# Two rows to a partition: 4 MB slots and transfers, half of the bias kept in PSUM

## The chip, the cores and the metric

The kernel runs on one core of a Trainium2 chip. Such a core has TensorE (PE, the matmul engine), VectorE (DVE), ScalarE (ACT) and GpSimd (POOL), the queues SP and ACT that issue transfers, and 16 DMA engines between HBM (the chip's main memory) and SBUF (the core's working memory, 128 partitions). PSUM is the small memory that TensorE writes. The metric is device microseconds (us), the median of several runs. All arithmetic is fp32.

## The reference

```python
B, D, L = (16384, 4096, 6)
x0 = inputs
def step(x, wb):
    wi, bi = wb
    xw = jnp.matmul(x, wi)          # (B, D) by (D, 1)
    x_new = x0 * xw + bi + x
    return (x_new, None)
x, _ = jax.lax.scan(step, inputs, (w, b))
```

Every layer's result has the form `x0 * s + c`, where `s` is one number for each row and `c` one vector for all rows. So a row needs its six dot products with the six weight vectors, a recurrence of six steps on `1 + dot` (with constants from weights and biases), and one pass `out = x0 * s_last + c_last`, where `c_last` is the sum of the six biases. 268 MB are read and 268 MB written.

## The kernel before

**Tiles and units.** The 16384 rows are 128 tiles of 128 rows; a row lies in one partition, so a tile is 128 x 4096 fp32, 2 MB, with 16 KB for each partition. SBUF has eight tile slots. Work goes in units: the first two tiles alone (`HEAD`), then 61 pairs, then four tiles alone (`TAIL`).

**A unit's steps.** VectorE transposes its tiles in 32 x 32 squares into `blocks`, which has four places of 128 x 2048 (L264); a pair is four pieces of 2048 columns, two pieces for each half of D. TensorE multiplies each piece with the weights into `dots` (L401 for pairs, L359 for single tiles). ScalarE copies `dots` into `spread` (L197), TensorE folds it into `turned` (L370), ScalarE adds 1 (`growth`, L205), VectorE runs the six-step recurrence (L275), and VectorE finishes each tile in place with one instruction over 4096 columns (L286). ScalarE's queue then stores the tile (L210; the last tile in quarters, L236).

**Order of the work.** All order is written out by hand. VectorE, for a pair u: transposes of pieces 0 and 1, the recurrence of u-1, finish of u-1's first tile, transposes of pieces 2 and 3, finish of u-1's second tile (L310 to L323). ScalarE stores u-1's first tile before it spreads u's dots, the second behind it (L218 to L230). SP issues the loads in order; from the ninth on, each waits until the store of the same slot has landed (L141). DVE waits for both tiles of a pair (L266). A transpose waits until TensorE has used the piece that was in its place of `blocks` four pieces ago (L261).

**The start.** Weights and biases land in the last slot. TensorE sums the biases into `scratch` (four PSUM banks) in two rounds, `sum_bias(0)` and `sum_bias(1)` (L337), by a matrix `quarter_sum` that ScalarE builds; ScalarE copies each round into `c_last` in SBUF (L187). SP's load for the last slot waits until this is done.

## Time and profile before

| | us |
|---|---|
| median of 3 runs (1281.14 to 1282.9) | 1281.35 |
| the profiled execution: its own time | 1280.2 |
| its span in the profile | 1278.4 |
| busy: DVE / PE / ACT | 1150.2 / 780.7 / 102.7 |
| mean DMA rate over the span | 420 GB/s |
| TensorE clock granted (share of full speed) | 0.782 |

Busy time is summed over the instructions of an engine. The span begins with the first instruction and ends with the last event; what lies around it is 1.8 us here. The DMA share of a stretch is the mean busy share of the 16 DMA engines; it can read slightly above 1 since the records of two packets that follow each other overlap a little. A packet is the contiguous piece that one DMA engine moves as one record: here one row of 16 KB, or 4 bytes for the semaphore that tells of the landing.

### The profile page before, as it was taken

The numbers are of one execution on the slowest core, as the hardware profiler recorded it, in microseconds if no ns is written. First come the engines' busy times: TensorE is split into PE (matmuls) and PEld (weight loads), VectorE is DVE, ScalarE is ACT, GpSimd is POOL, SyncE is SP. The second block draws the span as 40 slices with busy tenths as digits, with TensorE's granted clock in tenths as the row PEclk, the third lists the DMA queues.
The fourth block names the chain that finished last, engine by engine and source line by source line (L and its number), as shares of the span: only waits on it lengthen the run. The fifth ranks groups of instructions, "written<-read, shape, count | busy, mean of one in ns | idle before, by whom it ended". The sixth has DMA issues, their size and how long they took to land.

```text
span 1278.4 us, 20057 instructions
## 1 busy us (share of the span) xinstructions
PE 780.7 (61%) x9114; PEld 728.6 (57%) x9114; DVE 1150.2 (90%) x526; ACT 102.7 (8%) x345; POOL 4.3 (0%) x17
## 2 busy tenths in 40 slices
PE   8666666555656655556555665665655665665653
PEld 4666566555556655555545565565655654665653
DVE  5999999898988988989889898898998988989896
ACT  3000000000000000000000000000000000000010
POOL 1000000000000000000000000000000000000000
PEclk9877787887877778778787777777777778678677
DMA  9999999999999999999999999999999999999996
GB/s 385 416 380 428 430 431 431 429 427 429 433 429 431 431 430 432 430 431 424 421 424 425 418 427 421 424 425 422 427 424 421 424 423 425 425 423 425 426 421 286
DMA packets 37385, 537.28 MB, mean 420 GB/s; under 512 B 4168, under 2 KB 4168, under 8 KB 4728
## 3 DMA queue, kind: packets, MB, share of 16 engines
q1 hardware_dynamic: 18432, 268.44, 50.1%
q10 hardware_dynamic: 18936, 268.64, 49.3%
q8 instruction: 7, 0.11, 0.0%
q14 instruction: 10, 0.08, 0.0%
HBM read 268.63 MB, written 268.44 MB: 420 GB/s over the span
## 4 chain that ended last, share of the span: by engine, by line
DMA 72%; DVE 15%; PE 8%; issue 3%; ACT 1%; DVEq 0%
DMA out_dram<-tiles 56%; DMA tiles<-in_r_inputs_dram 15%; DVE tiles L286 8%; DVE blocks L264 7%; PE dots L401 6%; ACT spread L197 1%; PE dots L359 1%; PE scratch L339 1%; DMA tiles<-in_L_rec_w_dram 0%; PE strips L334 0%; PE strips L349 0%; ACT c_last L189 0%; PE turned L370 0%; DVE scale L275 0%; DVEq L42 0%
## 5 line engine op out<-in xcount | busy, mean ns | idle before, releaser
L401 PE MATMUL dots<-blocks,weights 128*64 128x128 f32 x7808 | 662.6, 349 | 380.8 <-DVE blocks L264 380.6
L401 PEld LDWEIGHTS dots<-blocks,weights 128*64 128x64 f32 x7808 | 628.7, 185 | 405.3 <-DVE blocks L264 405.2
L264 DVE STREAM_TRANSPOSE blocks<-tiles 128x2048 f32<-128x2048 f32 x256 | 576.0, 2288 | 100.1 <-issue 100.1
L286 DVE SCALAR_TENSOR_TENSOR tiles<-tiles,scale,c_last 128x4096 f32<-128x4096 f32 (+1 forms) x131 | 571.9, 4368 | 0.2
L197 ACT ACTIVATE spread<-dots,group_mask 128x128 f32<-128x128 f32 (+1 forms) x268 | 75.2, 363 | 1062.6 <-PE dots L401 1020.3
L370 PE MATMUL turned<-layer_sel,spread 128*128 128x8 f32 x512 | 68.1, 258 | 85.5 <-ACT spread L197 85.5
L370 PEld LDWEIGHTS turned<-layer_sel,spread 128*128 128x128 f32 x512 | 62.3, 191 | 101.4 <-issue 95.6
L359 PE MATMUL dots<-blocks,weights 128*64 128x64 f32 x768 | 32.4, 266 | 11.0 <-DVE blocks L264 11.0
L359 PEld LDWEIGHTS dots<-blocks,weights 128*64 128x64 f32 x768 | 31.7, 180 | 12.9 <-issue 12.9
L205 ACT ACTIVATE growth<-turned,ones 128x16 f32<-128x16 f32 (+1 forms) x67 | 18.3, 273 | 85.0 <-PE turned L370 85.0
L275 DVE TENSOR_TENSOR_SCAN scale<-growth,cw 128x6 f32<-128x6 f32 x128 | 13.3, 142 | 8.9 <-ACT growth L205 8.9
L339 PE MATMUL scratch<-tiles,quarter_sum 24*128 24x512 f32 x16 | 10.7, 825 | 0.0
L339 PEld LDWEIGHTS scratch<-tiles,quarter_sum 24*128 24x128 f32 x16 | 4.0, 253 | 5.7 <-issue 4.8
L334 PE MATMUL strips<-tiles,copies 24*128 24x512 f32 x4 | 3.7, 1085 | 5.6 <-DMA tiles<-in_L_rec_w_dram 5.6
L291 DVE STREAM_TRANSPOSE tiles<-strips 128x1024 f32<-128x1024 f32 x1 | 1.2, 1249 | 5.5 <-PE strips L334 5.5
L334 PEld LDWEIGHTS strips<-tiles,copies 24*128 24x128 f32 x4 | 1.2, 318 | 6.6 <-issue 6.6
L189 ACT COPY c_last<-scratch 128x2048 f32<-128x2048 f32 x2 | 3.7, 1866 | 5.4 <-PE scratch L339 5.4
L302 DVE CUSTOM_DVE_ANT_0 tiles<-strips,tiles 24x1024 f32<-24x1024 f32 x1 | 1.2, 1212 | 2.7 <-PE strips L349 2.7
L349 PE MATMUL strips<-tiles,earlier 24*24 24x512 f32 x4 | 3.6, 1052 | 0.0
L183 ACT COPY weights<-tiles 32x768 f32<-32x768 f32 x2 | 3.0, 1520 | 4.6 <-DVE tiles L291 4.6
L349 PEld LDWEIGHTS strips<-tiles,earlier 24*24 24x24 f32 x4 | 0.5, 138 | 2.9 <-issue 2.9
L244 DVE MEMSET weights<- 128x2048 f32 x1 | 1.8, 1765 | 0.4 <-issue 0.4
(25 smaller groups left out, 11.3 us busy)
## 6 DMA issues: line engine op xcount, KB each, us to landing
tiles<-in_r_inputs_dram SPq DMA_DIRECT2D x128, 2048.0 KB, 14.9
out_dram<-tiles ACTq DMA_DIRECT2D x127, 2048.0 KB, 25.5
out_dram<-tiles ACTq DMA_DIRECT2D x4, 512.0 KB, 7.0
tiles<-in_L_rec_w_dram ACTq DMA_DIRECT2D x1, 96.0 KB
tiles<-in_L_rec_b_dram ACTq DMA_DIRECT2D x1, 96.0 KB
```

Source lines behind the costliest of these rows:

```text
L189: nc.scalar.copy(c_halves[:, :, h, :], scratch[:]).then_inc(scratch_copied, 1)
L197: nc.scalar.activation(spread[:, 0:n_of, :, g, :], dots[:, 0:n_of, :, :], ACT.Copy, scale=group_mask[:, g:g + 1]).then_inc(dots_spread, 1)
L205: nc.scalar.activation(growth[:, 0:n_of, :], turned[:, 0:n_of, :], ACT.Identity, bias=ones[:, 0:1]).then_inc(growth_ready, 1)
L264: nc.vector.transpose(blocks[:, p % PLACES, :], source).then_inc(blocks_ready, 1)
L275: nc.vector.tensor_tensor_scan(scale[:, u % 2, t, 0:L], growth[:, t, 0:L], cw[:, 0:L], 1.0, ALU.mult, ALU.add).then_inc(scale_ready, 1)
L286: nc.vector.scalar_tensor_tensor(out=tiles[:, s, at], in0=tiles[:, s, at], scalar=scale[:, u % 2, t, L - 1:L], in1=c_last[:, at], op0=ALU. ...
L334: nc.tensor.matmul(strips[:, k, :], copies[0:STRIPS, :, :], strips_w[:, k * BANK:(k + 1) * BANK], start=True, stop=True).then_inc(w_copied, 1)
L339: last = nc.tensor.matmul(scratch[:, j, :], quarter_sum[0:STRIPS, j, :], strips_b[:, h * BANK:(h + 1) * BANK], start=True, stop=True)
L349: nc.tensor.matmul(strips[0:STRIPS, k, :], earlier[0:STRIPS, 0:STRIPS], strips_b[:, k * BANK:(k + 1) * BANK], start=True, stop=True).then_ ...
L359: last = nc.tensor.matmul(dots[at:at + KM * Q, 0, :, :], weights[:, h * PIECE // Q + k:h * PIECE // Q + k + KM, :], blocks[:, p % PLACES, ...
L370: last = nc.tensor.matmul(turned[:, t, :], spread[:, t, m, :, :], layer_sel[:, m, :], start=(m == 0), stop=(m == KM - 1))
L401: last = nc.tensor.matmul(dots[at:at + KM * Q, :, :, :], weights[:, c * CH // Q + k:c * CH // Q + k + KM, :], place[:, :, k * Q:(k + KM) * Q],
```

## The change

A slot now holds two tiles: row 2p of a group of 256 rows lies in partition p beside row 2p+1. So partition p reads and writes 32 KB that are contiguous in HBM, and a pair is one load and one store of 4 MB. There are five slots of 4 MB in place of eight of 2 MB. To make room, `blocks` shrinks from four places to two, and of `c_last` only the lower half of the columns stays in SBUF (`c_low`); the upper half is left in `scratch` in PSUM (`c_high`) and read from there. The finish of a tile is therefore two instructions of 2048 columns. The six tiles that go alone are still loaded and stored alone, 16 KB to a partition. ScalarE stores a whole unit, behind the growth of the next one. The biases come by four small DMAs into the partitions where TensorE sums them with `ones` (no `quarter_sum`), and `strips_b` comes last.

```diff
-PLACES = 4
+PLACES = 2
+PIECES_OF_PAIR = 4
-N_SLOTS = 8
+N_SLOTS = 5
...
+    x_pairs = x.rearrange("(q p t) d -> q p t d", p=P, t=TB)
+    out_pairs = out.rearrange("(q p t) d -> q p t d", p=P, t=TB)
+    b_halves = b.rearrange("l (h j n) -> j l h n", h=2, j=G)
...
-        tiles = sb("tiles", [P, N_SLOTS, D])
+        tiles = sb("tiles", [P, N_SLOTS, TB, D])
-        c_last = sb("c_last", [P, D])
+        c_low = sb("c_low", [P, HALF])
+        c_high = scratch[:].rearrange("p j n -> p (j n)")
...
+            for q in range(n_all_pairs):
+                s = q % N_SLOTS
+                if q == N_SLOTS - 1:
                     sp.wait_ge(weights_ready, G)
-                    sp.wait_ge(scratch_filled, 2)
+                    sp.wait_ge(bias_summed, 2)
                     sp.wait_ge(strips_summed, 1)
...
+                if q >= N_SLOTS:
+                    for t in range(TB if in_singles(q - N_SLOTS) else 1):
+                        sp.wait_ge(y_stored[s][t], 16 * transfers(q - N_SLOTS, t))
+                if in_singles(q):
+                    for t in range(TB):
+                        sp.dma_start(tiles[:, s, t, :], x_pairs[q, :, t, :]).then_inc(x_landed[s][t], 16)
+                else:
+                    sp.dma_start(tiles[:, s, :, :], x_pairs[q]).then_inc(x_landed[s][0], 16)
...
             act.dma_start(strips_w, w_strips).then_inc(w_landed, 16)
-            act.dma_start(strips_b, b_strips).then_inc(b_landed, 16)
...
+                act.dma_start(b_rows[j * Q:j * Q + L, :, :], b_halves[j]).then_inc(b_landed[j], 16)
+            act.dma_start(strips_b, b_strips).then_inc(strips_b_landed, 16)
...
+            act.wait_ge(bias_summed, 1)
+            nc.scalar.copy(c_low[:], c_high).then_inc(c_low_ready, 1)
...
             for u in range(1, n_units):
...
-                    store(first)
-                    spread_dots(u)
-                    for t in range(1, n_of):
-                        store(first + t)
-                    make_growth(u)
+                spread_dots(u)
+                make_growth(u)
+                store(u - 1)
...
-                parts = 1 if n < n_tiles - 1 else PIECES
+                parts = 2 if n < n_tiles - 1 else STORE_PARTS
...
+                    c = c_low[:, at] if i < parts // 2 else c_high[:, i * width - HALF:(i + 1) * width - HALF]
+                    done = nc.vector.scalar_tensor_tensor(out=tile[:, at], in0=tile[:, at],
+                                                          scalar=scale[:, u % 2, t, L - 1:L], in1=c,
+                                                          op0=ALU.mult, op1=ALU.add)
```

The first listing is the ACT queue before: from the first stores on through one pair of the long middle part (L210 stores, L197 spreads, L205 makes the growth).

```order
L205 ACTIVATE growth<-turned,ones 128x8
L210 DMA out_dram<-tiles 128x4096 x2
L197 ACTIVATE spread<-dots,group_mask 128x4x32 x4
L205 ACTIVATE growth<-turned,ones 128x16
L210 DMA out_dram<-tiles 128x4096
L197 ACTIVATE spread<-dots,group_mask 128x4x32 x4
L210 DMA out_dram<-tiles 128x4096
L205 ACTIVATE growth<-turned,ones 128x16
```

The second is the same place now: L223 stores a single tile, L221 a pair.

```order
L212 ACTIVATE growth<-turned,ones 128x8
L223 DMA out_dram<-tiles 128x4096
L202 ACTIVATE spread<-dots,group_mask 128x4x32 x4
L212 ACTIVATE growth<-turned,ones 128x16
L223 DMA out_dram<-tiles 128x4096
L202 ACTIVATE spread<-dots,group_mask 128x4x32 x4
L212 ACTIVATE growth<-turned,ones 128x16
L221 DMA out_dram<-tiles 128x8192
```

The store of tile 1 has moved behind the spread and the growth of the first pair, and each pair's two stores are one, behind the next unit's growth.

The third listing is DVE before, one pair of the middle part (L264 transposes, L275 the recurrence, L286 finishes).

```order
L264 STREAM_TRANSPOSE blocks<-tiles 128x2048 x2
L275 SCALAR_TENSOR_TENSOR scale<-growth,cw 128x6 x2
L286 SCALAR_TENSOR_TENSOR tiles<-tiles,scale,c_last 128x4096
L264 STREAM_TRANSPOSE blocks<-tiles 128x2048 x2
L286 SCALAR_TENSOR_TENSOR tiles<-tiles,scale,c_last 128x4096
```

And DVE now, the same pair (`scratch` is the upper half of the bias in PSUM).

```order
L268 STREAM_TRANSPOSE blocks<-tiles 128x2048 x2
L279 SCALAR_TENSOR_TENSOR scale<-growth,cw 128x6 x2
L291 SCALAR_TENSOR_TENSOR tiles<-tiles,scale,c_low 128x2048
L291 SCALAR_TENSOR_TENSOR tiles<-tiles,scale,scratch 128x2048
L268 STREAM_TRANSPOSE blocks<-tiles 128x2048 x2
L291 SCALAR_TENSOR_TENSOR tiles<-tiles,scale,c_low 128x2048
L291 SCALAR_TENSOR_TENSOR tiles<-tiles,scale,scratch 128x2048
```

The order of transposes and finishes stays; each finish has become two instructions, the second with an operand in PSUM.

## Rows read from the trace of the kernel before

**Rows 1.** Windows: stretch, busy us by engine, TensorE clock, DMA share, GB/s.

```profile
0.00:5.00 5.00, 0.00 (x0) 0.00 (x0) 2.56 (x5) 1.53 (x2) 3.71 (x14) 1.00 0.52 187
...
2.00:36.00 34.00, 29.16 (x290) 16.78 (x290) 19.25 (x16) 11.62 (x20) 3.03 (x8) 1.00 0.99 410
60.00:90.00 30.00, 18.99 (x230) 17.60 (x228) 30.00 (x14) 2.83 (x10) 0.00 (x0) 0.82 0.95 374
160.00:560.00 400.00, 242.94 (x2792) 229.86 (x2792) 364.21 (x165) 28.57 (x101) 0.00 (x0) 0.78 1.01 430
560.00:1240.00 680.00, 409.92 (x4721) 388.24 (x4723) 615.69 (x276) 49.29 (x175) 0.00 (x0) 0.77 1.01 424
1250.00:1278.40 28.40, 9.31 (x222) 8.88 (x218) 18.07 (x10) 2.39 (x10) 0.00 (x0) 0.74 0.65 268
```

**Rows 2.** Timeline, one pair in the middle: start, length, engine, line, idle before.

```profile
610.64 4.50 DVE L264 STREAM_TRANSPOSE blocks<-tiles 128x2048 f32<-128x2048 f32 x2 [1.93 <-issue]
613.00 6.44 PE L401 MATMUL dots<-blocks,weights 128*64 128x128 f32 x64 [3.38 <-DVE blocks L264]
615.23 4.49 DVE L286 SCALAR_TENSOR_TENSOR tiles<-tiles,scale,c_last 128x4096 f32<-128x4096 f32 x1
619.63 4.50 DVE L264 STREAM_TRANSPOSE blocks<-tiles 128x2048 f32<-128x2048 f32 x2
621.99 5.38 PE L401 MATMUL dots<-blocks,weights 128*64 128x128 f32 x64 [2.55 <-DVE blocks L264]
...
629.78 0.27 ACT L205 ACTIVATE growth<-turned,ones 128x16 f32<-128x16 f32 x1 [1.22 <-PE turned L370]
630.44 4.51 DVE L264 STREAM_TRANSPOSE blocks<-tiles 128x2048 f32<-128x2048 f32 x2 [1.94 <-issue]
```

**Rows 3.** Page, part 6: transfers, count, KB, median us to landing.

```profile
tiles<-in_r_inputs_dram SPq DMA_DIRECT2D x128, 2048.0 KB, 14.9
out_dram<-tiles ACTq DMA_DIRECT2D x127, 2048.0 KB, 25.5
```

**Rows 4.** DMA queues from 1269 to 1273 us, where 4 KB packets run.

```profile
DMA packets 392, 1.48 MB, mean 370 GB/s; under 512 B 46, under 2 KB 46, under 8 KB 387
q10 hardware_dynamic: 392, 1.48, 92.7%
```

**Rows 5.** Groups by line and shape: busy us, mean ns of one.

```profile
L264 DVE STREAM_TRANSPOSE blocks<-tiles 128x2048 f32<-128x2048 f32 x256 | 576.0, 2288 | 100.1 <-issue 100.1
L291 DVE STREAM_TRANSPOSE tiles<-strips 128x1024 f32<-128x1024 f32 x1 | 1.2, 1249 | 5.5 <-PE strips L334 5.5
L302 DVE CUSTOM_DVE_ANT_0 tiles<-strips,tiles 24x1024 f32<-24x1024 f32 x1 | 1.2, 1212 | 2.7 <-PE strips L349 2.7
L286 DVE SCALAR_TENSOR_TENSOR tiles<-tiles,scale,c_last 128x1024 f32<-128x1024 f32 x4 | 4.9, 1280 | 0.0
```

**Rows 6.** Timeline of the start: first stores, first pair's spread and recurrence.

```profile
36.69 9.36 ACTq L210 DMA_DIRECT2D out_dram<-tiles  x2
53.35 1.14 ACT L197 ACTIVATE spread<-dots,group_mask 128x128 f32<-128x128 f32 x4 [17.29 <-PE dots L401]
56.13 0.24 DVE L275 TENSOR_TENSOR_SCAN scale<-growth,cw 128x6 f32<-128x6 f32 x2 [1.68 <-ACT growth L205]
60.85 0.34 ACTq L210 DMA_DIRECT2D out_dram<-tiles  x1
69.64 0.34 ACTq L210 DMA_DIRECT2D out_dram<-tiles  x1
```

**Rows 7.** Timeline of the end: last pair's transposes, last two finishes, last stores.

```profile
1204.86 4.50 DVE L264 STREAM_TRANSPOSE blocks<-tiles 128x2048 f32<-128x2048 f32 x2 [1.96 <-issue]
1258.58 4.48 DVE L286 SCALAR_TENSOR_TENSOR tiles<-tiles,scale,c_last 128x4096 f32<-128x4096 f32 x1
1264.12 4.87 DVE L286 SCALAR_TENSOR_TENSOR tiles<-tiles,scale,c_last 128x1024 f32<-128x1024 f32 x4
1265.43 4.23 ACTq L236 DMA_DIRECT2D out_dram<-tiles  x4
```

More of the change, by code:

```diff
@@ L120, in tiles_of, with in_singles, transfers @@
             return u + n_pairs * (TB - 1), 1
+        def in_singles(q):
+            return q * TB < HEAD or q * TB >= n_tiles - TAIL
         def pieces_before(u):
             return 2 * tiles_of(u)[0]
+        def transfers(q, t):
+            return sum(1 for k in range(q % N_SLOTS, q + 1, N_SLOTS) if t == 0 or in_singles(k))
         def weights_of(g):
@@ L206, in make_growth, with store @@
                                      bias=ones[:, 0:1]).then_inc(growth_ready, 1)
-            def store(n):
-                act.wait_ge(tiles_done, n + 1)
-                act.dma_start(out[n * P:(n + 1) * P, :], tiles[:, n % N_SLOTS, :]).then_inc(y_stored[n % N_SLOTS], 16)
-            keep_bias(0)
-            spread_dots(0)
-            keep_bias(1)
+            def store(u):
+                first, n_of = tiles_of(u)
+                q, t = first // TB, first % TB
+                s = q % N_SLOTS
+                act.wait_ge(tiles_done, first + n_of)
+                if n_of == TB:
+                    act.dma_start(out_pairs[q], tiles[:, s, :, :]).then_inc(y_stored[s][0], 16)
+                else:
+                    act.dma_start(out_pairs[q, :, t, :], tiles[:, s, t, :]).then_inc(y_stored[s][t], 16)
@@ L215, in _ @@
             act.wait_ge(cw_all_ready, 1)
             nc.scalar.copy(cw[:], strips[:, 0, 0:LP]).then_inc(cw_ready, 1)
+            spread_dots(0)
             make_growth(0)
             for u in range(1, n_units):
[L219 to L230 removed]
@@ L232, in _ @@
-            for i in range(PIECES):
-                n = n_tiles - 1
-                at = slice(i * PW, (i + 1) * PW)
-                act.wait_ge(tiles_done, n + i + 1)
-                act.dma_start(out[n * P:(n + 1) * P, at], tiles[:, n % N_SLOTS, at]).then_inc(y_stored[n % N_SLOTS], 16)
-            for s in range(N_SLOTS):
-                last_stores = 1 if s < N_SLOTS - 1 else PIECES
-                act.wait_ge(y_stored[s], 16 * (n_rounds - 1 + last_stores))
+                spread_dots(u)
@@ new lines, in _ @@
+                make_growth(u)
+                store(u - 1)
+            last_slot = (n_all_pairs - 1) % N_SLOTS
+            for i in range(STORE_PARTS):
+                at = slice(i * D // STORE_PARTS, (i + 1) * D // STORE_PARTS)
+                act.wait_ge(tiles_done, n_tiles + i)
+                act.dma_start(out_pairs[n_all_pairs - 1, :, TB - 1, at],
+                              tiles[:, last_slot, TB - 1, at]).then_inc(y_stored[last_slot][TB - 1], 16)
+            for q in range(n_all_pairs - N_SLOTS, n_all_pairs):
+                s = q % N_SLOTS
+                act.wait_ge(y_stored[s][0], 16 * transfers(q, 0))
+                if transfers(q, 1) > 0:
+                    parts = STORE_PARTS if q == n_all_pairs - 1 else 1
+                    act.wait_ge(y_stored[s][1], 16 * (transfers(q, 1) - 1 + parts))
@@ L395, in _ @@
                 pe.wait_ge(dots_spread, n * G + (HEAD - 1) * G)
-                for c in range(PLACES):
-                    pe.wait_ge(blocks_ready, n * PLACES + c + 1)
-                    place = blocks[:, c, :].rearrange("p (t n) -> p t n", t=TB)
+                for c in range(PIECES_OF_PAIR):
+                    pe.wait_ge(blocks_ready, n * PIECES_OF_PAIR + c + 1)
+                    place = blocks[:, c % PLACES, :].rearrange("p (t n) -> p t n", t=TB)
                     for k in range(0, CH // Q, KM):
```

102 lines of the change are left out of this document (40 added, 62 removed).

## The prediction

> **What bounds the kernel now.** I read the windows first, for DMA share and GB/s by stretch [rows 1]. From 160 to 1240 us the DMA engines are busy all the time (share 1.01), at 430 GB/s up to 560 us and 424 after it. DVE, at 90% of the span, looks like a rival, but the timeline of one pair settles it [rows 2]: DVE's pairs start at 610.64 and 630.44, 19.80 us apart, and before each it stood idle for 1.93 or 1.94 us although growth was ready (629.78 plus 0.27 is before 630.44) and the places were free; it waited for the load. DVE works 17.86 us in a pair. A pair is 8.39 MB both ways, and 8.39 MB in 19.80 us is 424 GB/s, the window's number. So the middle is bound by the DMA rate, and DVE has 1.94 us to spare per pair. Only two stretches lose much: 60 to 90 us at 374 GB/s, and the last 28.4 us at 268 [rows 1].
>
> In the end stretch DVE sets the pace: from the last pair's transposes at 1204.86 to the last finish (1264.12 + 4.87) it is never idle for long, and the last quarter's store closes the span 9.4 us behind it [rows 7].
>
> **Term 1, longer packets.** Per engine a 16 KB packet takes 16384 x 16 / 430e9 = 609.6 ns at the undisturbed rate [rows 1]. For 4 KB packets: 392 records, 46 of them semaphores and 5 of 16 KB, leave 341; busy time is 4 us x 16 x 0.927 = 59.3 us, less 5 x 0.61 and the semaphores (taken as 9 ns, the sum cares little), 55.9 us, so 164 ns, some 4 less for overlapping records (share 1.01): 160 ns [rows 1, 4]. The line through both is 36.6 ns per KB and 9.7 ns fixed. The fixed part can't be much more than this; the records of one stretch with few packets may mislead by some ns, so I take 7.5. An engine moves 256 tiles x 8 = 2048 packets; halving them, but for the six single tiles each way, takes away 976: 976 x 7.5 = 7.3 us. 122 DMAs fewer take as many semaphore packets from each engine, about 1 us. Together -8.4. Bounds: 0 (the packets stay 16 KB, or the fixed part isn't per packet) and 976 x 9.7 + 1 = -10.5. A 32 KB packet is in no row.
>
> The Trainium skill (DMA: Bandwidth & Descriptors, "Why small descriptors are slow") gives a fixed cost of about 3 cycles per packet inside the engine and calls merging worthwhile only for tiny descriptors. With that page's 850 MHz it is 3.5 ns, and this term would be 3.4 us. The rows lean to more than twice that, from few packets.
>
> **Term 2, the second stretch's rate.** 680 us at 424 where 430 was to be had is 680 x (1 - 424/430) = 9.5 us [rows 1]. The share is 1.01 in both, so single packets grew longer there. Loads land 14.9 us after issue, stores 25.5 [rows 3], and a load is only issued once its slot's store has landed, so the load queue often runs out and starts anew. A slot's round after the change: from DVE's start on a pair to its store 19.5 + 19.4 = 39 us (its own turn, and the next pair's up to ScalarE's growth, which ends 629.78 + 0.27 - 610.64 = 19.4 into a turn [rows 2]), store 19.5, load 19.5, two starts of about 2 us: 82. Five slots at 19.5 us are 97.5, so loads are asked for some 15 us before they could run, while before it was 79.2 (four pairs at 19.8) with nothing left over. I take half of the loss back: -5. Bounds: -9.5, and on the other side the lower rate from the start (400 us at 424: +5.6).
>
> **Term 3, the start.** Tile 1's store was issued at about 45.7 us (two stores from 36.69 over 9.36) [rows 6]. It now stands behind spread and growth of the first pair, done at 56.1 [rows 6]; that pair's last pieces must be transposed and multiplied first. Until then the DMAs have five pairs of loads and tile 0's store, 11 tiles x 4.85 us = 53.4 us, from about 2.4 on (5 us at a share of 0.52 [rows 1]): to 55.8. Slot 0 is reloaded when both its stores have landed: some 2 us idle before tile 1's packets flow, 4.9 us for them, 2 idle again. The first pair's store comes at about 70 (before: its two tiles at 60.85 and 69.64 [rows 6]), and once its bytes and the reload are through (65 + 4 x 4.85 = 84.4) another 2 us pass. That is 6 to 7 us, against 30 x (1 - 374/430) = 3.9 us lost there before [rows 1]. Six small DMAs on ACT in place of two, interleaved with the loads, can hold up the first dots by 2 to 4 us, of which the deeper stock of loads hides most. +4; bounds 0 and +9.
>
> **Term 4, VectorE.** A finish in two parts: four quarters took 4.87 us where one piece takes 4.48 [rows 7], so an instruction more costs 0.13 us. The PSUM operand: the transpose of 1024 columns out of PSUM took 1249 ns, half of the 2048-column one from SBUF is 1144 with half of its fixed cost [rows 5]; the two-input instruction with one input in PSUM took 1212 against 1280 for the finish of 1024 columns, all in SBUF. So no slower rate, at most 0.1 us each. A pair costs 17.86 + 2 x 0.13 + 2 x 0.03 to 0.1 = 18.2 to 18.3 us. The DMA's pair of 19.4 covers it with 1.1 us to spare; without that cover it would be 0.4 x 64 = 26 us. Two places in `blocks` in place of four: pieces 0 and 1 are multiplied by 613.00 + 6.44 = 619.44, just before piece 2 is transposed at 619.63 [rows 2], and it needs only piece 0. Pieces 2 and 3 are through at 627.4, before the next transposes. Nothing, but for singles: first and last units, under 0.5 us each.
>
> **Term 5, the end.** DVE's path over the last pair and four singles gains six finishes x 0.16 = +1. But one whole pair's store is then outstanding behind the last load, and there the DMAs were 35% idle (268 GB/s) [rows 1]: bytes moved from the full stretch into the idle one, about one tile, 4.9 us less before it and 2 more in it. Sum -2; bounds -5 and +3.
>
> **The sum.** Against the span of 1278.4: -8.4 - 5 + 4 + 0 - 2 = 1267.0. The profiled execution took 1.8 us more than its span, 1268.8, and the median of the runs is 1.15 above it: 1270.
>
> The Trainium skill (SBUF — State Buffer, "The DMA setup-cost knee") puts about 2 us on each DMA and advises the largest single transfer. Taken as a cost in series, 122 fewer would save 244 us. The rows speak against it: the share of 1.01 leaves no 2 us gap, the costs overlap.
>
> **The rivals.**
> - *Packets bring nothing.* The packets stay 16 KB, or the fixed part lies elsewhere, while slots and order change as said. For it: the 9.7 ns hang on 341 packets of the last stores. Terms 2, 3 and 5 remain: 1270 + 8.4 = 1278; if the reads don't recover either, 1283. The skill's page above on small descriptors leans this way. Chance 0.17.
> - *Longer reads disturb more.* Slower. A read that stalls holds its engine; with 32 KB turns for both queues and rows 128 KB apart between engines, the 1.4% loss of the second stretch could double and hold from the start: rate 418. 537 MB at 418 in place of a mean near 429 is 1285 - 1252 = +33, so about 1300. It decides from a rate of 424 on, where terms 1 and 2 turn to +6 and the time is about 1284. For it: 374 GB/s at a share of 0.95 from 60 to 90 [rows 1], where stalls cost more than idleness. Against: 430 for 400 us. Chance 0.11.
> - *VectorE becomes the bound.* Slower. The PSUM operand costs more than the rows show. It decides from 19.8 - 18.1 = 1.7 us per pair, 0.85 us for each half; at 1 us each 62.5 x 0.3 = +19, 1300; at half the rate (2.1 us each) 1281 + 62.5 x 2.5 = 1437. Against: both PSUM rows [rows 5]. Chance 0.05.
>
> **Numbers.** My forecast, 1270 with 1262 to 1277 of its own, has 0.67. 0.2% is 2.6 us, about what a measurement of this kernel tells from no change. Faster: 0.67 plus a third of the first rival, 0.72. Within: 0.12, nearly all from the first rival. Slower: 0.16, from the last two. The range for 8 in 10 goes from 1260 (both first terms full) to 1284.
>
> **What would show it.** In the changed profile: main queues with some 9000 data packets each in place of 16384; 431 GB/s or more in the middle; pairs on DVE 19.4 to 19.5 us apart with 1 us idle; finishes of 2048 columns at 2.3 us, the PSUM one at most 0.1 longer; two or three gaps in the DMA share between 55 and 90 us; an end stretch like before. Wrong would be: a rate of 424 or less in the middle (the second rival), DVE never idle in the middle, or waits of DVE's transposes for TensorE.

## The result and the profile after

The change makes the kernel slower: 1290.85 us median (1288.29 to 1291.89, 4 runs) against 1281.49 of before in the same session (1281.14 to 1282.9, 4 runs), ratio 1.0068 with a 95% interval of 1.0051 to 1.0085. Forecast were 1270 us, with 1260 to 1284 as the range; the chance given to a slower kernel was 0.16. The profiled execution took 1288.29 us, its span is 1286.3, 7.9 more than before's.

Windows of the kernel after, columns and stretches as in [rows 1] (the stretch 90 to 110 is new, the last one goes to the new end):

```profile
0.00:5.00 5.00, 0.00 (x0) 0.00 (x0) 2.34 (x4) 0.00 (x0) 3.71 (x14) 1.00 0.67 206
2.00:36.00 34.00, 26.63 (x290) 14.52 (x290) 21.13 (x17) 8.74 (x15) 3.03 (x8) 0.99 1.00 406
60.00:90.00 30.00, 20.84 (x226) 19.95 (x228) 30.00 (x16) 2.84 (x10) 0.00 (x0) 0.73 0.88 360
90.00:110.00 20.00, 14.65 (x168) 14.08 (x166) 20.00 (x14) 1.42 (x5) 0.00 (x0) 0.76 1.00 393
160.00:560.00 400.00, 246.50 (x2802) 233.48 (x2804) 373.00 (x208) 28.36 (x100) 0.00 (x0) 0.78 1.00 433
560.00:1240.00 680.00, 405.46 (x4687) 384.04 (x4685) 618.90 (x343) 49.42 (x175) 0.00 (x0) 0.77 1.00 420
...
1250.00:1286.30 36.30, 13.09 (x264) 12.69 (x264) 23.37 (x15) 2.40 (x10) 0.00 (x0) 0.70 0.64 269
```

The rate rises to 433 GB/s up to 560 us, as forecast, and then falls further than before, to 420 against 424. The packets of the two main queues (part 3 of the page), and below them the transfers with their median us to landing (part 6, answering to [rows 3]):

```profile
q1 hardware_dynamic: 9648, 268.44, 50.2%
q10 hardware_dynamic: 10224, 268.74, 48.6%
```

```profile
tiles<-in_r_inputs_dram SPq DMA_DIRECT2D x61, 4096.0 KB, 24.7
out_dram<-tiles ACTq DMA_DIRECT2D x61, 4096.0 KB, 35.3
```

The packets are 32 KB. The finish on DVE, by shape (mean ns of one behind the busy time), and what DVE waited for (us, times, longest):

```profile
L291 DVE SCALAR_TENSOR_TENSOR tiles<-tiles,scale,scratch 128x2048 f32<-128x2048 f32 x127 | 297.4, 2342 | 0.0
L291 DVE SCALAR_TENSOR_TENSOR tiles<-tiles,scale,c_low 128x2048 f32<-128x2048 f32 x127 | 296.2, 2332 | 0.2
```

```profile
DVE blocks L268 <- DMA tiles<-in_r_inputs_dram: 97.0, 52, 4.6
...
DVE blocks L268 <- PE dots L411: 1.4, 1, 1.4
```

The operand in PSUM costs 10 ns. The small `blocks` costs 1.4 us once in the pairs. DVE waits 52 times for a load; it is not the bound.

Where the 7.9 us are, the timeline of DVE shows: a pair in the middle, the last pair, and the last two single tiles (start, length, idle before):

```profile
625.95 2.31 DVE L268 STREAM_TRANSPOSE blocks<-tiles 128x2048 f32<-128x2048 f32 x1 [1.83 <-DMA tiles<-in_r_inputs_dram]
...
645.64 2.31 DVE L268 STREAM_TRANSPOSE blocks<-tiles 128x2048 f32<-128x2048 f32 x1 [1.59 <-DMA tiles<-in_r_inputs_dram]
...
1205.41 2.31 DVE L268 STREAM_TRANSPOSE blocks<-tiles 128x2048 f32<-128x2048 f32 x1 [1.84 <-DMA tiles<-in_r_inputs_dram]
...
1250.51 4.50 DVE L268 STREAM_TRANSPOSE blocks<-tiles 128x2048 f32<-128x2048 f32 x2 [4.24 <-DMA tiles<-in_r_inputs_dram]
...
1264.36 4.50 DVE L268 STREAM_TRANSPOSE blocks<-tiles 128x2048 f32<-128x2048 f32 x2 [4.65 <-DMA tiles<-in_r_inputs_dram]
```

The last pair begins at 1205.41, 0.55 us later than before [rows 7]; from there to the end are 80.9 us against 1278.4 - 1204.9 = 73.5. So the packets' gain has vanished by the last pair, and 7.4 us are lost behind it. Two waits for single tiles stand there, which before did not have; whether they are the cause is tested below ("The end").

### The profile page after: what moved, and what is told of

It is laid out like the page before. It is cut to its first block, busy times and chain, and to the rows that moved or that the text cites. A ratio compares the mean times of both kernels' runs of the same rounds, so it can differ in the third digit from the quotient of the medians.

```text
span 1286.3 us, 20063 instructions
## 1 busy us (share of the span) xinstructions
PE 783.3 (61%) x9114; PEld 732.1 (57%) x9114; DVE 1165.9 (91%) x652; ACT 100.1 (8%) x340; POOL 4.3 (0%) x17
## 4 chain that ended last, share of the span: by engine, by line
DMA 64%; DVE 26%; PE 7%; issue 1%; ACT 1%; ACTq 0%; DVEq 0%; SPq 0%
DMA out_dram<-tiles 36%; DMA tiles<-in_r_inputs_dram 27%; DVE blocks L268 14%; DVE tiles L291 11%; PE dots L411 5%; PE turned L380 1%; ACT spread L202 1%; DMA tiles<-in_L_rec_b_dram 1%; PE dots L369 1%; PE strips L359 0%; DVE scale L279 0%; ACTq L185 0%; DVEq L46 0%; ACT growth L212 0%; ACTq L183 0%
## 5 line engine op out<-in xcount | busy, mean ns | idle before, releaser
L291 DVE SCALAR_TENSOR_TENSOR tiles<-tiles,scale,scratch 128x2048 f32<-128x2048 f32 x129 | 299.9, 2326 | 0.0
L291 DVE SCALAR_TENSOR_TENSOR tiles<-tiles,scale,c_low 128x2048 f32<-128x2048 f32 x129 | 298.7, 2316 | 0.2
L369 PE MATMUL dots<-blocks,weights 128*64 128x64 f32 x768 | 32.8, 267 | 20.1 <-DVE blocks L268 20.1
L349 PE MATMUL scratch<-tiles,ones 6*128 6x512 f32 x16 | 9.0, 876 | 0.2
L298 DVE STREAM_TRANSPOSE tiles<-strips 128x1024 f32<-128x1024 f32 x1 | 1.2, 1250 | 6.2 <-PE strips L342 6.2
L349 PEld LDWEIGHTS scratch<-tiles,ones 6*128 6x128 f32 x16 | 2.6, 245 | 5.5 <-DMA tiles<-in_L_rec_b_dram 4.4
```

What stands on the lines that cost most here:

```text
L291: done = nc.vector.scalar_tensor_tensor(out=tile[:, at], in0=tile[:, at], scalar=scale[:, u % 2, t, L - 1:L], in1=c, op0=ALU.mult, op1=ALU ...
L349: last = nc.tensor.matmul(scratch[:, j, :], ones[j * Q:j * Q + L, :], b_rows[j * Q:j * Q + L, h, :], start=True, stop=True, tile_position= ...
L369: last = nc.tensor.matmul(dots[at:at + KM * Q, 0, :, :], weights[:, h * PIECE // Q + k:h * PIECE // Q + k + KM, :], blocks[:, p % PLACES, ...
```

## The experiments

Times are medians; ratios are to the kernel before on the same chip. Where times of two experiments are subtracted, they can come from different chips: before took 1280.7 to 1282.3 us on them, so such a difference is good to about 1 us.

### Is it the long packets, the memory or the slots?

**rotated**: before, with the rows' order turned by half, to see whether the slow stretch is a place in HBM.

```diff
-x[n * P:(n + 1) * P, :]
+x[row(n):row(n) + P, :]      # row(n) = (n + n_tiles // 2) % n_tiles * P; the same for out
```

> The kernel before, with the order of the tiles turned by half: first tiles 64 to 127, then 0 to 63, in loads and stores alike. It asks why the middle falls from 430 to 424 GB/s at about 560 us in the kernel before and from 433 to 420 in the changed one. Theory A (the place in HBM): reads are slower in some part of the input (from about tile 59 on). Then the slow stretch lies at the start, up to some 640 us (near 424 GB/s or less), the fast one (430) behind it; the total stays within 3 us of before. Theory B (how the engines' queues drift apart with time, or time itself): the slow stretch begins at about 560 us again, whatever the tiles.

Measured: 1281.2 us, ratio 0.9991 (0.997 to 1.0013). 430 GB/s from 160 to 560 us, 423 after it, as before. The slow stretch keeps its time, not its place.

**short_packets**: after, but a partition's two rows lie 128 rows apart, so the transfers stay 4 MB with packets of 16 KB.

```diff
-x_pairs = x.rearrange("(q p t) d -> q p t d", p=P, t=TB)      # and out_pairs
+x_pairs = x.rearrange("(q t p) d -> q p t d", p=P, t=TB)
```

> The changed kernel with one edit: a partition holds rows p and p + 128 of its group of 256 in place of 2p and 2p + 1. Loads and stores are still 4 MB, slots, PSUM half and queue order as changed, but packets are 16 KB again. Theory A (long packets make the read stalls dearer): 560 to 1240 us runs at 424 GB/s or more in place of 420, 160 to 560 us at 430 in place of 433; time 1283 to 1287, 4 to 8 us under the changed kernel. Theory B (the big transfers and the later stores are what costs): 560 to 1240 us stays at 420 and the time at 1288 to 1293 or above.

Measured: 1281.59 us, ratio 0.9989 (0.9969 to 1.0009), 431 and 424 GB/s. All of the loss comes with the long packets (or with what the edit changes besides, which rows lie side by side in a partition); slots, order, PSUM and the one store per pair cost nothing together.

**ten_slots**: the memory part alone, ten slots of one tile, every tile its own transfer.

```diff
 def in_singles(q):
-    return q * TB < HEAD or q * TB >= n_tiles - TAIL
+    return True               # with the mapping of short_packets; stores in before's order
```

> The memory part of the change alone: ten slots of one tile, two places in blocks, upper half of the bias in PSUM, finishes in two halves; but loads and stores by the tile (2 MB, 16 KB packets) and in the order of the kernel before (first tile of a pair stored early). Theory A (long packets are the loss): 1276 to 1282, as before or a little better, since the DMAs set the pace and two slots more can only help at the start; 424 GB/s from 560 to 1240 us. Theory B (the slots or VectorE's four extra halves are the loss): 1286 or more.

Measured: 1280.28 us, ratio 0.9981 (0.9958 to 1.0004), 431 and 425 GB/s, as Theory A had it. One of its ten executions took 1504.24 us, which nothing here explains.

**four_slots**: the transfer part alone, four slots of 4 MB, as much memory as before's eight of 2 MB.

```diff
-N_SLOTS = 8                   # of one tile
+N_SLOTS = 4                   # of two tiles, 32 KB packets; all of c_last kept
```

> The transfer part of the change alone: four slots of 4 MB with 32 KB packets both ways (the same SBUF as before), four places in blocks, the whole bias in SBUF, finishes in one piece; stores as changed, one per pair behind the next growth. Theory A (long packets are the loss, by dearer read stalls): 418 to 421 GB/s from 560 to 1240 us and 433 before it; 1290 to 1297, the fifth slot having helped little. Theory B (slots are the loss): the round of a slot, 39 us of work and a store and a load at half rate, takes 82 us where four slots give 78; so about 82/4 = 20.5 us for a pair, 1315 to 1330, and DMA share clearly below 1.

Measured: 1333.9 us, ratio 1.0383 (1.0331 to 1.0435), 410 and 408 GB/s, a pair every 20.6 us. That is Theory B, 4 us above its range: four slots of 4 MB are too few for the round of load, work and store; the fifth is what makes this form of transfer bearable.

### What are the transfers alone capable of?

**moves_16k, moves_32k**: loads and stores through slots, no computation at all (the output is the input).

```diff
-LONG = False                  # eight slots of 2 MB, 16 KB packets
+LONG = True                   # four slots of 4 MB, 32 KB packets
```

> Transfers alone: the 128 tiles are loaded (2 MB each, 16 KB packets, eight slots) and stored again, with no computation; the output is the input. It asks what holds a pair at 19.8 us in every kernel so far although the mean rate of the first half is 430 GB/s, by which a pair takes 19.5. Theory A (one of the 16 DMA engines is some 2% slower than the others; a transfer has landed when its last engine is done, so this engine sets the pace once the others have used up their lead): 64 x 19.8 + 5 to 10 = about 1273 to 1278, mean rate 421 to 424, the last engines landing well behind the first. Theory B (the round of the slots through DVE, PE and ACT sets it): without that round the mean rate holds, 537 MB at 430 = 1249 + 5 to 10 = 1254 to 1260.

> Transfers alone, two rows to a partition: 64 loads and stores of 4 MB with 32 KB packets, four slots of 4 MB (the same SBUF as in the 16 KB run); no computation, the output is the input. Theory A (the slow engine's handicap is its rate, not a cost per packet, so longer packets give it next to nothing): within 3 us of the 16 KB run. Theory B (the fixed part of a packet, 5 to 10 ns by the rows, is saved on every engine): 7 to 8 us less than the 16 KB run. A third outcome, longer by more than 5 us, would say that long packets hurt the reads by themselves.

Measured: 1252.29 us (1252.1 to 1253.14), ratio 0.977, and 1246.3 us (1245.69 to 1246.4), ratio 0.9722 (0.9706 to 0.9738). GB/s in 40 slices of the span (part 2 of the page), moves_16k:

```profile
GB/s 385 431 433 429 432 430 433 430 432 432 430 433 429 432 431 432 431 432 431 430 434 428 432 431 431 432 432 432 429 432 430 433 430 432 432 430 433 429 432 399
```

No slow stretch. Long packets do save, 6.0 us, and do no harm by themselves. The computing kernel is 29 us slower than the pure transfers, with a DMA share of 1.01 as well; where these 29 us go is asked further down.

**moves_split**: moves_16k with every 32nd tile moved as 120 and 8 partitions, a try to find a slow DMA engine.

```diff
-SPLIT_EVERY = 0
+SPLIT_EVERY = 32
```

> Transfers alone as in the 16 KB run, but of every 32nd tile (4 of 128) the rows go as two DMAs, 120 partitions and 8, both ways. 120 partitions divide by 15 and not by 16, so by the Trainium skill (DMA: Bandwidth & Descriptors, the section on why a DMA increments its semaphore by 16) engine 15 gets nothing of them, and the eight rows go to engines 0 to 7. Engine 15 has 3% less to do, engines 0 to 7 0.4% more. If the slow engine is the last one: 64 x 19.5 to 19.6 + 5 to 10, some 13 to 17 us less than the 16 KB run. If it is one of 0 to 7: 5 us more. If it is one of 8 to 14, or there is none: within 2 us, with a few us for the uneven transfers themselves.

Measured: 1275.42 us, ratio 0.9952 (0.9935 to 0.9968). It settles nothing on engines: four split tiles cost 23.1 us, 5.8 each, more than any outcome that the expectation had for a slow engine. The one row more that the 8 partitions would put on eight of the engines is 4 x 2 x 0.61 = 4.9 us of it; where the rest goes was not looked into.

### The end

**pair_loads_at_end**: after, with the last four tiles loaded as two pairs. **short_stores_at_end**: after, with the last eight pairs stored in 16 KB packets.

```diff
-if in_singles(q):             # pair_loads_at_end: separate loads
+if q * TB < HEAD:
-if n_of == TB:                # short_stores_at_end: one store
+if n_of == TB and stored_apart(q):   # the last 8 pairs: two stores of one tile
```

> The changed kernel with one edit: the last four tiles, still computed and stored one by one, are loaded two at a time like the pairs (4 MB, 32 KB packets) in place of one at a time (2 MB, 16 KB packets). In the changed kernel the stretch from the last pair's first transpose to the end took 80.9 us, 7.4 more than before, with waits of 4.2 and 4.7 us for the loads of the last two tiles. Theory A (an engine takes a packet of each queue in turn, so loads in 16 KB packets beside stores in 32 KB packets get a third of the rate instead of half): the waits shrink, the end stretch falls to 74 to 77 us and the time by 4 to 7 us to 1284 to 1287. Theory B (the end is later because more stores are outstanding there): nothing changes, 1289 to 1292, since the same bytes are outstanding.

> The kernel after, but the last eight pairs are stored as two transfers of 16 KB packets each, so that the single tiles at the end are loaded beside stores whose packets are as long as theirs. Theory A (the end costs 7.4 us more than before since an engine that takes packets in turn gives 16 KB loads a third beside 32 KB stores): the last two single tiles no longer wait 4 us each, the stretch from the last pair to the end is 73 to 76 us instead of 80.9, time 1283 to 1286 us. Theory B (the end is long since the store queue is deeper): 79 to 81 us, 1289 to 1292 us.

Measured: 1292.98 us, ratio 1.0094 (1.0074 to 1.0113), and 1292.9 us, ratio 1.01 (1.0074 to 1.0126). In its profile the first had the short end (76.1 us after the last pair's start, 1282.16 us in all), but its other runs lay at 1292 to 1297. The second has no wait of DVE for its last tiles any more, and an end of 82.2 us. So Theory A is refuted as the cause: the waits of the last tiles go with the mixed packets, the time does not. That the deeper store queue (Theory B) is the cause is not shown by this either.

### What in the computation costs 29 us?

**moves_dve**: moves_16k beside 505 transposes on memory of their own. **moves_finish**: two transposes and one in-place operation on DVE between load and store. **moves_pe**: moves_16k beside TensorE's loop, on memory of its own. TensorE's and ScalarE's part is left out of the first two, VectorE's and ScalarE's of the third, and the output is the input.

```diff
+for i in range(505): nc.vector.transpose(blocks[:, i % 2, :], blocks[:, 2 + i % 2, :])   # moves_dve
+nc.vector.transpose(blocks..., tiles[:, s, ...]); nc.vector.scalar_tensor_tensor(out=tiles[:, s, :], ...)  # moves_finish
+with pe.Fori(0, 62) as n:     # moves_pe: 64 matmuls a turn, as L401
```

> Question: 16 KB transfers alone took 1252.3 us at 431 GB/s throughout, the kernel before falls to 424 in its second stretch and its pairs are 19.8 us apart instead of 19.5. What of the computation does that? Here VectorE runs 505 transposes of 2048 columns (about 1160 us, which is its whole work of the kernel before) on memory of its own beside the same transfers, with no wait between the two. Theory A (VectorE's traffic on SBUF slows the transfers): 424 to 428 GB/s, 1262 to 1275 us. Theory B (the transfers are held by the coupling, a store that can only be issued when the work on its slot is done and a load that waits for that store): 431 GB/s and 1252 +-2 us.

> Transfers of 16 KB packets, and VectorE alone between load and store: two transposes and one operation in place per tile (about 9.1 us a tile, as in the kernel before), TensorE and ScalarE's arithmetic left out; the output is x with a zero added. Theory B (the coupling holds the pair pace): pairs 19.8 us apart, 424 GB/s in 560-1240, 1272 to 1282 us. Theory A' (TensorE or ScalarE beside the transfers): 430 GB/s or more throughout, pairs 19.5 apart, 1258 to 1264 us.

> The same with TensorE's loop in VectorE's place (62 turns of 64 matmuls of 256 columns, weights loaded as in the kernel before), on memory of its own, without a wait between it and the transfers. Theory A' (TensorE's reads or its instruction traffic slow the transfers): 420 to 428 GB/s, 1262 us or more. Theory B: 431 GB/s and 1252 +-2 us. The results of the computation are not stored.

Measured: moves_dve 1254.45 us, moves_finish 1254.98, moves_pe 1272.36 (1271.95 to 1272.61); ratios 0.9786, 0.9792 and 0.9925 (0.9909 to 0.9942). VectorE with its whole work, coupled to the slots, costs 2.7 us. TensorE beside the transfers, with no wait between them, costs 20.1. (Its matmuls have 128 moving columns, as in the kernel; the 256 of the expectation is a slip.) Windows of moves_pe (busy PE, PEld and POOL, then clock, share, GB/s), and its queues from 1228 to 1258 us, packets and share of 16 engines:

```profile
60.00:430.00 370.00, 370.00 (x6784) 370.00 (x6780) 0.00 (x0) 1.00 1.01 430
500.00:1200.00 700.00, 0.00 (x0) 0.00 (x0) 0.00 (x0) 0.50 1.01 431
1228.00:1258.00 30.00, 0.00 (x0) 0.00 (x0) 0.00 (x0) 0.50 0.56 236
```

```profile
q10 hardware_dynamic: 470, 6.67, 52.5%
q1 hardware_dynamic: 28, 0.41, 3.2%
```

The mean rate hardly differs while TensorE runs (to 446 us) and not at all after it. But in the tail, loads (q1) take 3.2% of sixteen engines, and half of one engine is 1/32 = 3.1%: one engine is still reading, in turn with its writes, while the others have no read left: in the packet records nearly all reads of this tail start 1.21 to 1.22 us apart, and a read or a write takes 0.61.

The landings show the same engine's lag directly. Every load raises its semaphore 16 times, once for each engine's part. Time from the first of these to the fifteenth and to the sixteenth, medians in us by stretch, worked out from the semaphore events of the traces:

```
                60-160      160-360     360-560     560-900     900-1200
moves_16k       0.9  0.9    0.9  0.9    0.9  0.9    0.9  1.5    0.9  1.5
moves_pe        1.8  5.3    3.5 18.6    3.5 35.2    2.9 37.8    3.5 38.6
moves_pe_wide   0.7  1.3    0.7  3.1    1.0  7.0    1.4 15.7    2.0 19.4
```

In moves_pe fifteen parts land within 3.5 us and the sixteenth ever later, as long as TensorE runs (to 446 us); after that its lag hardly changes. Without TensorE there is no late part. So one engine falls behind beside TensorE and never catches up, and every tile waits for it, since each has a part on all sixteen. The records carry no engine number; that it is the same one each time follows from a lag that is far longer than one pair and grows steadily. (The third row is the next experiment; TensorE runs to 870 us there.)

**moves_pe_wide**: the same columns through TensorE in half the instructions.

```diff
-KM = 2                        # 64 matmuls a turn, weights of 64 columns, 128 moving columns
+KM = 4                        # 32 matmuls a turn, 128 and 256
```

> The transfers of 16 KB packets beside TensorE's loop again, with the same columns through the array in half the instructions: weight blocks of 128 columns and 256 moving columns in place of 64 and 128, so 32 matmuls a turn and not 64. Transfers beside TensorE took 1272.4 us against 1252.3 alone, and in the tail of that trace one DMA engine was still loading for 35 us after the other fifteen had no more loads. Theory C (that one engine carries TensorE's stream of instructions too, and falls behind with their number): about half of the 20 us goes, 1260 to 1264 us. Theory D (TensorE's reads of SBUF slow that engine; the columns it reads are the same): 1270 to 1274 us.

Measured: 1263.37 us (1263.08 to 1263.71), ratio 0.9852 (0.9811 to 0.9893). 11.1 us of loss in place of 20.1, and half the lag of the last part (19.4 us in place of 38.6), with the same columns: it goes with the number of TensorE's instructions, Theory C. One more thing differs: TensorE's loop lasts 858 us in place of 436, so its reads come at half the pace. That the pace is not what counts, the kernel before shows further down: it has 272 records in 19.8 us where moves_pe has 256 in 7.0, and loses 0.33 us in that time, moves_pe 0.32.

### Does it hold the full kernel?

**wide_dots_before, wide_dots_after, wide_ten**: before, after and ten_slots with KM = 4.

```diff
-KM = 2
+KM = 4
```

> The kernel before with KM = 4: the same sums in half the matmuls of the dots (32 of 256 moving columns to a pair), four times the work of `turn` and twice the columns of the spread. Theory C (one DMA engine, slowed by TensorE's instructions, sets the pairs' pace of 19.8 us): pairs 19.6 to 19.7 us apart, no slow second stretch or a later one, 1268 to 1274 us. Theory D: 1280 to 1283 us, as before.

> The kernel after with KM = 4. Theory C (one slow DMA engine sets the pace and is also what the last single tiles wait for, so that the packets' saving never reaches the end): 1265 to 1278 us, the loss of 9 us against before at least halved when both have the wider matmuls. Theory D: 1288 to 1292 us. A chain of matmul, spread and turn that becomes too long for VectorE would show as waits of its transposes for TensorE or of its scans for ScalarE, and over 1290 us.

> The memory part alone (ten slots of one tile, transfers of one tile each in 16 KB packets, bias half in PSUM), which took 1280.3 us, with KM = 4. It is meant as the version that beats both. Theory C: 1264 to 1273 us. Theory D: 1279 to 1282 us.

Measured: 1289.43 us (1284.16 to 1296.53), 1289.79 (1284.88 to 1297.35) and 1287.26 (1281.41 to 1292.05); ratios 1.0064, 1.006 and 1.0043. The first and the third lie above what either theory gave, the second where Theory D had it. But the expectation's own proviso came true. The dots' group of wide_dots_after, and its waits:

```profile
L411 PE MATMUL dots<-blocks,weights 128*128 128x256 f32 x3904 | 943.8, 406 | 11.2 <-DVE blocks L268 11.2
```

```profile
DVE blocks L268 <- PE dots L411: 62.8, 61, 1.7
DVE scale L279 <- ACT growth L212: 24.6, 38, 5.7
```

TensorE's dots take 944 us in place of 666, and DVE waits for TensorE 61 times and nowhere for a load (wide_ten likewise). Of the block products of a matmul only those on the diagonal are needed, one in two with KM = 2, one in four here. The bound has moved to TensorE, so these times tell nothing for or against either theory. What the second and third lose, they lose at the start (wide_dots_after's 19th pair begins at 391.9 us, after's at 369.0); from there their pairs are the fastest of all that compute, 19.46 and 19.53 us, and no load is late. wide_dots_before does still wait for its loads, 40 times (the profile puts such waits of the kernel before down to "issue"), so its pace can be read: 19.71 us a pair, just outside the 19.6 to 19.7 of Theory C, against 19.81 of before, and 426 GB/s from 560 to 1240 us. Its waits for loads:

```profile
DVE blocks L264 <- issue: 70.3, 40, 2.5
```

**alternate_ten, alternate_after**: ten_slots and after, with every second pair from the eighth on in wide matmuls.

```diff
+def km_of(u):                 # 4 for every second pair from the eighth on, else 2
-with pe.Fori(1, n_pairs + 1) as n:
+with pe.Fori(0, NARROW_PAIRS) as n:
+    pair(n, KM)
+with pe.Fori(0, (n_pairs - NARROW_PAIRS) // 2) as n:
+    pair(n * 2 + NARROW_PAIRS, WIDE)
+    pair(n * 2 + (NARROW_PAIRS + 1), KM)
```

> The memory part alone (ten slots, 16 KB packets, 1280.3 us) with every second pair's dots in half the matmuls (32 of 256 moving columns) from the eighth pair on, the others as before. With all pairs so, TensorE was busy for 90% of the time, VectorE's transposes waited for it, and runs lay between 1281 and 1292 us; alternating, it is busy for about 75% and should not be waited for. Theory C (one DMA engine, slowed by TensorE's instruction stream, sets the pace): the start is that of ten slots, pairs about 19.65 us apart from there on, 1268 to 1275 us. Theory D (TensorE's reads, or something else of the coupling, sets it): 1279 to 1284 us.

> The kernel after (32 KB packets, 1290.9 us) with the same alternation. Theory C: pairs 19.6 to 19.7 us apart, the last pair begins at 1193 to 1200 us instead of 1205, and the engine left behind is less late at the end: 1272 to 1284 us. Theory D: 1288 to 1292 us.

Measured: alternate_ten 1275.74 us (1275.37 to 1276.83, 5 runs), ratio 0.9961 (0.9948 to 0.9974), the fastest kernel of the study that computes everything, 5.4 us below before and below all of its runs (1279.77 to 1283.55), 0.7 us above what Theory C gave and 3.3 below Theory D. Its interval overlaps that of ten_slots (0.9958 to 1.0004), so the part of the wide matmuls alone is not clear of noise there. alternate_after 1280.11 (1275.9 to 1289.76, 12 runs), ratio 0.9995 (0.9979 to 1.001): the change's loss of 9.4 us can no longer be measured, and this interval lies well below that of after (1.0051 to 1.0085). Windows of alternate_ten:

```profile
160.00:560.00 400.00, 310.41 (x2213) 273.32 (x2214) 376.29 (x208) 32.65 (x100) 0.00 (x0) 0.84 1.01 431
560.00:1200.00 640.00, 485.76 (x3502) 427.80 (x3502) 588.25 (x324) 54.10 (x165) 0.00 (x0) 0.83 1.01 430
```

The slow second stretch has gone (ten_slots had 425 GB/s there), with TensorE busier than before. The pace of the pairs, from the start of the 19th and of the last pair's transposes in each timeline, 42 pairs apart:

```
kernel             19th pair  last pair  per pair   PE records of the dots and turns per pair
before                372.8     1204.9     19.81     272
after                 369.0     1205.4     19.91     272
short_packets         369.8     1202.7     19.83     272
ten_slots             366.8     1201.0     19.86     272
alternate_ten         365.8     1196.2     19.77     216 in the mean
wide_ten              381.1     1201.2     19.53     160 (TensorE bound)
wide_dots_after       391.9     1209.3     19.46     160 (TensorE bound)
wide_dots_before      378.4     1206.1     19.71     160
moves_finish          371.2     1189.1     19.48     0
```

Records are matmuls and weight loads: 2 x (128 + 8) for a narrow pair, 2 x (64 + 16) for a wide one. moves_pe lost 20.1 / 62 = 0.32 us a turn; before lies 19.81 - 19.48 = 0.33 above moves_finish, and wide_dots_before 0.23, where 160 of 272 records would leave 0.19. Between ten_slots and none are 0.38 us; 216 of 272 records would leave 0.30 and 19.78, and 19.77 were measured. The expected 19.65 had left out the turns and the half of the pairs that stayed narrow. alternate_after's profiled execution was the slowest of its twelve runs (1289.76, last pair at 1206.1), so its pace can't be read for the median.

The spans of before and moves_finish differ by 1278.4 - 1252.6 = 25.8 us: 1.6 before the 19th pair, 14.2 in the 42 pairs, 10.0 behind the last one's start. The 14.2 are the slower pace. How much of the 10.0 comes from the late engine, and how much from TensorE's and ScalarE's own work on the last tiles, was not separated.

## Why the prediction was wrong

**The step that failed** is in "What bounds the kernel now": "So the middle is bound by the DMA rate", with 424 GB/s as "the window's number" for one pair. In [rows 1] the same kernel moves 430 GB/s up to 560 us, and its pairs are 19.8 us apart there too ((571.0 - 372.8) / 10). The mean of sixteen engines was 430, the pace was that of the slowest, 424: fifteen engines ran ahead of it, until the slots held nothing more for them, and from then on the mean is that of the slowest. That is what the second stretch is. The landings show it: time from the first engine's semaphore packet to the fifteenth and the sixteenth, medians in us, for the loads worked out from the packet records, for the stores from the semaphore events:

```
                160-360     360-560     560-900     900-1200
before          1.3  1.8    1.2  2.4    4.7  6.4    5.1  6.7
after           1.1  2.5    1.1  2.7    2.5  7.1    2.8  7.6
moves_finish    1.7  2.0    1.7  2.0    2.3  2.5    2.8  3.1
stores:
before          2.7  6.5    5.0 13.9    4.2 16.9    4.5 16.9
after           2.0  5.1    2.2 13.7    1.1 17.2    1.4 17.4
moves_finish    1.3  1.5    1.3  1.5    2.0  2.4    2.7  2.9
```

In after's loads, fifteen engines are within 2.8 us and the last one 4.8 behind them. In its stores and in before's, the last part comes later and later up to 560 us and then stays at some 17 us, which is when the slow stretch begins.

The fifteen do not stand idle in the records: the share stays 1.01, as the prediction noted. What the second stretch loses stands in its reads. Before 560 us, 3 of 5176 data reads of before took more than 10% over the median of 611 ns; from 560 to 1200 us it was 544 of 8289, some 10 us on each of the sixteen engines, and in after 645 of 4097, some 18 us (median 1213 ns). moves_16k has 2 such reads of 8431. Whether such a read holds the wait for a free slot, or reads are slowed by something else, is not shown.

The sum missed the span by 1286.3 - 1267.0 = 19.3 us. Terms 1 to 3 were to bring the last pair's start 9.4 us forward and it moved 0.55 back, with pairs 19.91 us apart in place of the forecast 19.4 to 19.5; Term 5 is the other 9.4.

**Term 1, longer packets (-8.4).** Right in kind. A 16 KB record takes 611 ns, a 32 KB one 1213, so 9 ns are fixed, where 9.7 were read and 7.5 taken (the two points of the prediction give 10.1, not 9.7). But records overlap, short ones more (share 1.007 and 1.003): by the rates from 560 to 1200 us, 431.3 and 433.2 GB/s, two 16 KB packets cost 1215.6 ns and one of 32 KB 1210.3, 5.3 apart. So the size per packet was taken too large, 7.5 in place of 5.3. The transfers alone gained 6.0 us for 1024 packets less on each engine and 128 transfers less. But the computing kernel gained nothing of it in the pairs' pace, which went from 19.83 us (short_packets) to 19.91, although the late engine's packets are long too (see what stays open). The Trainium skill (DMA: Bandwidth & Descriptors, "Why small descriptors are slow") gives about 3 cycles a packet. At that page's 850 MHz this would be an estimated 3.6 us for 1024; the run shows 6.0 in all, between the page and the forecast.

**Term 2, the second stretch (-5).** Wrong in kind. "15 us before they could run" was the slack of the slots. The chain of waits of the kernel after, one round from 624 to 685 us:

```profile
624.15 36.25 DMA out_dram<-tiles
660.40 0.02 issue
660.42 24.97 DMA tiles<-in_r_inputs_dram
685.38 0.02 issue
685.41 4.50 DVE blocks L268 x2
```

Store 36.3 and load 25.0 in place of 19.5 each: with the forecast's 39 us for DVE's part that is 100 us, where five pairs take 5 x 19.9 = 99.5, and no slack. The spare time did not sit in front of the load, it went into the store: its last part lands 17 us behind the other fifteen (table above), and only then is the slot free. And no free slot makes the late engine faster.

**Term 3, the start (+4).** Its parts came as forecast. The stores of tile 1 and of the first pair in after's timeline, answering to [rows 6]:

```profile
53.70 0.36 ACTq L223 DMA_DIRECT2D out_dram<-tiles  x1
...
69.74 0.34 ACTq L221 DMA_DIRECT2D out_dram<-tiles  x1
```

The time lost there is 30 x (1 - 360/433) + 20 x (1 - 393/433) = 6.9 us where 6 to 7 were worked out (from 90 us on it is not idleness, the share is 1.00). An earlier first unit paid some back; the 19th pair starts 3.8 us before that of the kernel before.

**Term 4, VectorE (0).** Right: from a pair's transposes to the last finish of its turn it takes 645.64 - 1.59 - 625.95 = 18.1 us, and still waits 1.6 to 1.8 us for the next load.

**Term 5, the end (-2).** +7.4. It assumed that DVE sets the pace there, as in [rows 7]. The queues of after from 1250 to 1264 us:

```profile
q10 hardware_dynamic: 257, 4.31, 72.2%
q1 hardware_dynamic: 10, 0.13, 2.2%
```

Again a single engine is still loading, and now it gives its reads a third of its time, 1/16 x 1/3 = 2.1%: one 16 KB read for each 32 KB write. In before the reads end by 1243 us (q1 0.0% from 1243 to 1253). In the packet records most of its reads start 1.8 to 2.0 us apart, one read and one write of 0.61 and 1.21 us, where moves_pe's were 1.2 apart. By the Trainium skill (DMA: Bandwidth & Descriptors, "Queues, rings and completion order") an engine goes round its queues packet by packet, where the page means groups of typically 9 to 17 descriptors. The turns of the trace agree, 3.2% with equal packets and 2.2% with these, but here they are mostly single records, not such groups. short_stores_at_end shows that this decides which wait is seen, not the time.

**The rivals.** "Packets bring nothing" had its mechanism wrong (they bring 6 us alone) and, at 1278, missed the time. "Longer reads disturb more" had the sign; its 424 GB/s and 1284 us were the nearest, and its loss did double in the second stretch (from 433 to 420 is 3.0%, where before lost 1.4%), in reads that the trace shows as longer. But the rate did not fall from the start, and moves_32k shows no disturbed read, so length alone does not do it. "VectorE becomes the bound" did not happen. The case that came true, one engine that is late beside TensorE and no less late with long packets, was not among them.

**What stays open.** Why long packets are not only useless but 9 us worse in the computing kernel (after against short_packets). In the profiled runs 2.7 us of it lie before the last pair and 3.2 behind it. That it shrinks with fewer of TensorE's instructions (alternate_after) points to the late engine, but does not say how. Whether the late engine loses more beside 32 KB packets was not tried: TensorE's loop beside moves_32k is the missing run. Open is also what of an instruction reaches the DMA engine. Every run here, the timed ones too, was recorded with its span, so the instruction's loading and the record it leaves for the profiler can't be told apart. The page's instruction queues hold 3 packets in moves_pe (q8 and q14), and no queue of it shows the profiler's records.

## What to carry to other kernels

A DMA share of 1.0 and a mean GB/s don't say that all engines are equal: take the pace from the starts of the consumer in the timeline, compare it with what the transfers alone reach, and ask how far the last of a transfer's parts lands behind the others, and in the last 30 us whether a queue's share is that of a single engine. A kernel bound by transfers pays for the number of TensorE's instructions even where TensorE idles 40% of the time: wider matmuls are worth trying, as far as TensorE itself has room; the best kernel here was 0.4% faster than before. And a saving that the transfers alone show, 6.0 us here, need not reach the kernel: it has to be measured beside the computation.

## What the hardware showed that was not expected

- TensorE's loop beside transfers, with nothing shared by the program: 20.1 us for 15,872 matmul and weight-load records, 11.1 for 7,936 records with the same columns. VectorE's 505 instructions cost 2.2 us.
- One engine of sixteen carries it: beside TensorE the last part of a load lands 38.6 us behind the first, the other fourteen within 3.5; and the loads in the tail take 3.2% of sixteen engines, where half of one is 3.1%.
- A tile split in 120 and 8 partitions costs 5.8 us more than a whole one.
- Reading one operand of VectorE's two-input operation from PSUM costs 10 ns in 2332.
